# Unread 512-column products on TensorE around attention's first maxima and ahead of its first scores

## The chip, the cores and the metric

One core of a Trainium2 chip runs the whole kernel. The metric is the device time of one execution in microseconds (us). TensorE's clock is granted at one of two levels, 2.4 GHz (written 1.00 in the profile) or 1.2 GHz (written 0.50).

## The reference

A transformer block with adaptive layer norm, in float32, on `x` of 2 x 2048 tokens by 256. `mod` holds shifts, scales and gates computed from a condition vector. Cut to what matters:

```
h = layernorm(x) * (1 + ca) + sa
qkv = h @ qkv_w.T + qkv_b            # 16 heads of 16, rotary q and k
attn = softmax(q @ k.T * 16 ** -0.5)  # per batch and head, 2048 x 2048
x = x + ga * ((attn @ v) @ proj_w.T + proj_b)
h = layernorm(x) * (1 + cb) + sb
x = x + gb * (one of 8 relu experts, chosen by argmax of the gate logits)(h)
```

The softmax is exact: each query's maximum over its 2048 keys is found before the exponentials are taken.

## The kernel before, in words

Stages follow one another in one program: `front` (layer norm folded into weights, q, k, v, rotary), `attention`, `tail` (projection, second norm, routing), `experts`. Every engine has its own instruction stream, written out in full in Python, and the streams meet in semaphores. Within TensorE's stream the order is the order of the code; nothing is reordered by a planner.

Attention goes over 32 steps (`STEPS`). A step is four heads by 512 queries. For each step three kinds of products run on TensorE.

- **Maxima pairs** (`pair_product`, L1092 to L1104): two products at once, of 50 rows by 128 queries by 512 keys, in the two halves of the array (rows 0 to 49 and 64 to 113), into one of two PSUM buffers `PM`. VectorE reduces each pair to its maxima (`reduce_pair`, L1241 to L1245). 32 pairs make a step (`PAIR_TILES`). The operands are fp32r (the keys and queries split in a high and a low part, which is why they have 50 rows).
- **Scores** (`score_pair`, L1081 to L1090): `PS = K.T Q` for 128 keys by 512 queries, shifted by the maxima, into one of three PSUM banks (`SBANKS`). ScalarE takes the exponential of each (`exp_tile`, L1208 to L1213).
- **Values** (`value_products`, L1125 to L1139): eight instructions of 128 rows by 32 columns by 256, four of which share the array.

In the steady loop (`step`, L1174 to L1195) TensorE issues, for each of the 32 half groups of a step: one score pair two groups ahead (`OVER`), one maxima pair for the next step, and half of a group's value products. "Half group" below means this unit.

Before the loop there is a prologue (L1158 to L1172), and this is where the change lies. It has no scores to run beside, since the first step's maxima aren't known yet:

1. 32 pairs for step 0, each waiting until VectorE has freed its buffer (`maxima`, L1160).
2. `turn_shifts` (L1116 to L1123): four 128-column products that transpose the maxima, after VectorE's last reduction (L1252) and three small operations of GpSimd (L979 to L986). ScalarE copies the result (L1206), and SyncE moves it into `QE` (L860).
3. 14 early pairs of step 1 (`2 * EARLY`), the second of which waits for ScalarE's copy (`shifts_out`, L1166).
4. The first eight scores (`OVER` = 2 groups), and then step 0.

A wait stands in front of the instruction in TensorE's own stream, so whatever is written behind it waits too. The prologue starts once the last of `front` has finished.

Of the kernel before, what the change touches and what calls it, by code (L numbers as in the profile page):

```python
# [14 lines left out]
P = 128  # L15
# [13 lines left out]
CH = 512  # L29
# [673 lines left out]
def attention(nc, g):  # L703
# [8 lines left out]
    SBANKS = 3  # L712
# [6 lines left out]
    with ExitStack() as ctx:  # L719
        sem = open_sem(ctx, nc, "att")  # L720
        sb, ps = open_mem(ctx, nc, "att")
        K, QM = g.K, g.QM
# [17 lines left out]
        PS = [ps(f"PS{i}", [P, CH]) for i in range(SBANKS)]  # L740
# [36 lines left out]
        def shift_at(r, last):  # L777

            return SHIFT_AT - 2 * (SHIFT_GROUP + 1 - KT + EARLY) if last and r >= BODY - 2 else SHIFT_AT
# [5 lines left out]
        def pair_bank(r, at):  # L785
            return (FIRST + (PAIR_TILES + 1) * r + at) % 2

        def pair_number(s, at, shift):

            return PAIR_TILES + 2 * EARLY + PAIR_TILES * s + at - (1 if at > shift else 0) + 1  # L790
# [289 lines left out]
        def _(pe):  # L1080
            def score_pair(s, r, kt, ab):  # L1081

                if kt == 0 and ab == 0:
                    pe.wait_ge(shifts_placed, 16 * HEADS * (s + 1))
                for hh in range(2):
                    i = HEADS * kt + 2 * ab + hh
                    pe.wait_ge(exps, score_tile(s, i) - since_bank(i) + HELD)
                    rows = slice(64 * hh, 64 * hh + ROWS)
                    nc.tensor.matmul(PS[score_bank(i)][:], K[r % BODY // CHUNKS][rows, ab, kt * P:(kt + 1) * P],  # L1089
                                     QE[r % 2][rows, ab, :], start=True, stop=True).then_inc(scores, 1)  # L1090

            def pair_product(bank, r, it, n):  # L1092

                qt, ab, kc, u = n // 8, n // 4 % 2, n % 4, (r % BODY) // CHUNKS
                if n == 0:
                    if r > 0:
                        pe.wait_ge(queries_split, 2 * (BODY * it + r))
                    if r > 0 and r % CHUNKS == 0:
                        pe.wait_ge(keys_split, 2 * (2 * it + r // CHUNKS))
                for hh in range(2):  # L1100
                    rows = slice(64 * hh, 64 * hh + ROWS)
                    last = nc.tensor.matmul(PM[bank][:, hh, :], QM[r % 2][rows, ab, qt * P:(qt + 1) * P],  # L1102
                                            K[u][rows, ab, kc * CH:(kc + 1) * CH], start=True, stop=True)
                last.then_inc(max_products, 1)  # L1104

            def next_pair(s, r, it, last, at, ahead, n):

                shift = shift_at(r, last)
                number = pair_number(s, at, shift)
                if at == shift + 2:  # L1110
                    pe.wait_ge(shifts_out, s + 2)
                else:
                    pe.wait_ge(maxima, number - (1 if at == shift + 1 else 2) + AHEAD)
                pair_product(pair_bank(r, at), r + ahead, it, n)

            def turn_shifts(s, bank, pairs):  # L1116

                pe.wait_ge(shifts_ready, s + 1)
                pe.wait_ge(maxima, pairs - 1 + AHEAD)
                for qt in range(4):  # L1120
                    last = nc.tensor.matmul(PM[bank][:, 0, qt * P:(qt + 1) * P], mt[:, qt, :], identity[:],
                                            start=True, stop=True)
                last.then_inc(max_products, 1)  # L1123
# [33 lines left out]

            pe.sem_inc(pv_groups, SLOTS)  # L1158
            for n in range(PAIR_TILES):
                pe.wait_ge(maxima, n - 1 + AHEAD)  # L1160
                pair_product(n % 2, 0, 0, n)
            pe.wait_ge(ident_set, 3)
            turn_shifts(0, PAIR_TILES % 2, PAIR_TILES)
            for n in range(2 * EARLY):
                if n == 1:
                    pe.wait_ge(shifts_out, 1)  # L1166
                else:
                    pe.wait_ge(maxima, PAIR_TILES + n - (0 if n == 0 else 1) + AHEAD)
                pair_product((PAIR_TILES + 1 + n) % 2, 1, 0, n)
            for kt in range(OVER):  # L1170
                for ab in range(2):
                    score_pair(0, 0, kt, ab)  # L1172

            def step(it, r, last):  # L1174
                s = BODY * it + r
                final = last and r == BODY - 1
                issued = 0
                for j in range(KT):
                    for ab in range(2):
                        if j < KT - OVER:  # L1180
                            score_pair(s, r, j + OVER, ab)
                        elif not final:
                            score_pair(s + 1, r + 1, j - KT + OVER, ab)
                        ahead = 1 if j < KT - EARLY else 2
                        if ahead == 1 and not final or ahead == 2 and not (last and r >= BODY - 2):
                            n = 2 * (j + EARLY) + ab if ahead == 1 else 2 * (j - KT + EARLY) + ab
                            next_pair(s, r, it, last, issued, ahead, n)
                            issued += 1
                        if j == SHIFT_GROUP and ab == 1 and not final:
                            turn_shifts(s + 1, pair_bank(r, issued), PAIR_TILES * (s + 1) + 2 * EARLY + issued)  # L1190
                            issued += 1
                        value_products(s, r, it, j, ab)
                        at = 2 * (KT * (r - BODY + 2) + j) + ab - 2 * (SHIFT_GROUP + 2)
                        if last and 0 <= at < TB * KD:
                            first_projection(at)  # L1195
# [902 lines left out]
```

## Time and profile before

| | us |
|---|---|
| median of three runs | 1895.42 |
| the three runs | 1895.1 to 1900.64 |
| the profiled execution | 1896.42 |
| its span | 1894.7 |

| engine | busy share of the span |
|---|---|
| TensorE (PE) | 94% |
| VectorE (DVE) | 88% |
| ScalarE (ACT) | 75% |
| GpSimd (POOL) | 30% |

The span is the time from the first to the last instruction that the profiler saw; 1.72 us of the profiled execution lie around it. The line PEclk of the page gives the granted clock in 40 slices of 47.4 us. The page's list of groups shows attention's four large ones: 1024 reductions on VectorE (1245.5 us), 2048 exponentials on ScalarE (1112.3 us), 8192 value products (655.7 us) and 2048 score products (535.1 us) on TensorE. Times in the views are counted from the start of the span. A modelled matmul lasts from its issue until its result is there, so neighbouring ones overlap; the distance of two starts says what one really occupies.

### The profile page before, as it was taken

What the parts mean: (1) busy time and instruction counts of PE and PEld (TensorE: products, weight loads), DVE (VectorE), ACT (ScalarE), POOL (GpSimd) and SP (SyncE); (2) the same over time, 40 slices, a digit from 0 to 9 for tenths busy, and PEclk for the clock granted to TensorE, in tenths of its full rate; (3) what the DMA queues carried; (4) which work ended last, traced back from release to release, by engine and by line L of the source; (5) the groups of instructions that cost most, each with busy time, mean ns of one, the idle gap of its engine ahead of it and who ended that gap; (6) DMA issues with size and microseconds to landing.
All of it is one profiled execution on the core that took longest, in us unless ns stands there. A gap on an engine that the chain in (4) does not pass through costs nothing. (4 is left out here: it accounts for less than half of the span.)

```text
span 1894.7 us, 38505 instructions
## 1 busy us (share of the span) xinstructions
PE 1789.8 (94%) x15332; PEld 894.8 (47%) x15332; DVE 1658.5 (88%) x1803; ACT 1414.9 (75%) x2642; POOL 566.1 (30%) x406
## 2 busy tenths in 40 slices
PE   7976999999999999999999999999999994899997
PEld 4542333333333333333333333333333364899997
DVE  6779799999999999999999999999997475688886
ACT  1330788888888888888888888888888641688885
POOL 1115411151224115213411521331182015344442
PEclk8985899999999999999999999999999985899999
DMA  6766012331151133115113212521113733788873
GB/s 195 230 166 128 25 47 68 65 77 48 48 117 59 59 68 73 47 62 102 62 56 72 68 48 71 93 67 50 48 50 128 215 125 131 259 279 275 273 241 108
DMA packets 142660, 208.57 MB, mean 110 GB/s; under 512 B 42442, under 2 KB 87789, under 8 KB 140688
## 3 DMA queue, kind: packets, MB, share of 16 engines
q1 hardware_dynamic: 130608, 178.92, 33.1%
q0 software_dynamic: 7520, 18.80, 3.5%
q10 hardware_dynamic: 4352, 8.39, 1.3%
q8 instruction: 121, 1.98, 0.4%
q14 instruction: 59, 0.48, 0.1%
HBM read 122.10 MB, written 73.06 MB: 103 GB/s over the span
## 5 line engine op out<-in xcount | busy, mean ns | idle before, releaser
L1245 DVE TENSOR_REDUCE att_mx<-att_PM 128x2 f32<-128x1024 f32 x1024 | 1245.5, 1225 | 70.5 <-PE att_PM L1102 63.6
L1213 ACT ACTIVATE att_probs<-att_PS 128x512 f32<-128x512 f32 x2048 | 1112.3, 596 | 191.2 <-PE att_PS L1089 152.9
L1135 PE MATMUL att_PV<-att_probs,att_VU 128*32 128x256 f32 x8192 | 655.7, 392 | 7.8 <-ACT keep_sums L1234 6.2
L1089 PE MATMUL att_PS<-att_QE,K 50*128 50x512 f32 x2048 | 535.1, 498 | 1.9 <-ACT att_probs L1213 1.8
L1102 PE MATMUL att_PM<-K,QM 50*128 50x512 f32 x2048 | 439.4, 413 | 22.4 <-DVE att_mx L1245 15.0
L1089 PEld LDWEIGHTS att_PS<-att_QE,K 50*128 50x128 f32 x2048 | 203.4, 184 | 433.6 <-ACT att_probs L1213 410.5
L1135 PEld LDWEIGHTS att_PV<-att_probs,att_VU 128*32 128x32 f32 x8192 | 162.7, 108 | 368.9 <-issue 201.8
L979 POOL CAST att_mh<-att_m 128x16 fp32r<-128x16 f32 x32 | 6.3, 198 | 807.2 <-DVE att_m L1252 807.2
L1102 PEld LDWEIGHTS att_PM<-K,QM 50*128 50x128 f32 x2048 | 206.4, 191 | 44.8 <-DVE att_mx L1245 36.5
L576 POOL TENSOR_TENSOR QM<-QS,QM 16x1024 fp32r<-16x1024 f32 x62 | 146.5, 2363 | 8.5 <-POOL QM L995 6.1
L567 POOL TENSOR_TENSOR K<-KS,K 16x4096 fp32r<-16x4096 f32 x14 | 125.2, 8944 | 1.8 <-POOL K L1006 1.3
L1859 ACT ACTIVATE KS<-ffn_psh,ffn_b 128x256 f32<-128x256 f32 (+1 forms) x184 | 77.8, 496 | 44.2 <-PE ffn_psh L1955 43.6
L1811 POOL DMA_INDIRECT out<-QS,all_X x43 | 56.3, 1308 | 151.6 <-DVE QS L1896 139.3
L1919 DVE TENSOR_TENSOR ffn_hid_lo<-KS,ffn_hid_hi 128x512 fp32r<-128x512 f32 (+1 forms) x92 | 60.1, 654 | 15.7 <-ACT ffn_hid_hi L1859 14.8
L1955 PE MATMUL ffn_psh<-QM,keep_w_hi 128*128 128x256 f32 (+1 forms) x384 | 67.9, 281 | 1.4 <-ACT QM L1845 1.4
L1955 PE MATMUL ffn_psh<-QM,K 128*128 128x256 f32 (+1 forms) x528 | 64.6, 282 | 1.6 <-DVE K L1901 1.6
L1955 PEld LDWEIGHTS ffn_psh<-QM,K 128*128 128x128 f32 x528 | 63.6, 191 | 1.8 <-issue 1.8
L1969 PE MATMUL ffn_psy<-K,ffn_hid_hi 128*128 128x256 f32 x336 | 61.9, 286 | 0.0
L492 PE MATMUL front_psq<-front_xT,front_wf 128*128 128x512 f32 x128 | 58.6, 612 | 2.6 <-issue 2.6
L245 ACT ACTIVATE front_qk<-front_psq,front_bias_qk 128x512 f32<-128x512 f32 x32 | 22.0, 687 | 52.0 <-PE front_psq L492 52.0
L1955 PEld LDWEIGHTS ffn_psh<-QM,keep_w_hi 128*128 128x128 f32 x384 | 59.8, 194 | 1.8 <-ACT QM L1845 1.8
L1859 ACT ACTIVATE ffn_hid_hi<-ffn_psh,ffn_b 128x256 fp32r<-128x256 f32 (+1 forms) x138 | 58.2, 496 | 0.0
(217 smaller groups left out, 1598.9 us busy)
## 6 DMA issues: line engine op xcount, KB each, us to landing
H<-in_w SPq DMA_DIRECT2D x44, 1024.0 KB
routed_rows<-att_filling SPq DMA_DIRECT2D x32, 1088.0 KB, 4.3
att_QE<-QM SPq DMA_DIRECT2D x32, 512.0 KB, 3.1
QS<-qkT SPq DMA_DIRECT2D x186, 64.0 KB, 2.4
KS<-qkT SPq DMA_DIRECT2D x42, 256.0 KB, 9.0
qkT<-KS ACTq DMA_DIRECT2D x16, 512.0 KB, 4.9
all_X<-routed_rows SPq DMA_DIRECT2D x20, 258.0 KB
all_X<-in_x SPq DMA_DIRECT2D x4, 1024.0 KB, 9.8
```

What stands on the lines that cost most here:

```text
L492: last = nc.tensor.matmul(psq[:, odds, which, :], wf[b][:, k, n * P:(n + 1) * P], xT[q % 2][:, k, :], start=k == 0, stop=k == KD - 1)
L567: nc.gpsimd.tensor_tensor(keys[rows, :, :], stage[rows, :, :], keys[rows, :, :].bitcast(F32), ALU.subtract).then_inc(done, 1)
L576: nc.gpsimd.tensor_tensor(queries[rows, :, :], stage[rows, :, :], queries[rows, :, :].bitcast(F32), ALU.subtract).then_inc(done, 1)
L1089: nc.tensor.matmul(PS[score_bank(i)][:], K[r % BODY // CHUNKS][rows, ab, kt * P:(kt + 1) * P], QE[r % 2][rows, ab, :], start=True, stop=Tr ...
L1102: last = nc.tensor.matmul(PM[bank][:, hh, :], QM[r % 2][rows, ab, qt * P:(qt + 1) * P], K[u][rows, ab, kc * CH:(kc + 1) * CH], start=True, ...
L1135: last = nc.tensor.matmul(PV[32 * h:32 * h + VW, cols], VU[r // CHUNKS % 2][:, j, h, :], probs[:, j % SLOTS, h, cols], start=j == 0 and ha ...
L1213: nc.scalar.activation(probs[:, kt % SLOTS, h, :], PS[score_bank(i)][:], ACT.Exp).then_inc(exps, 1)
L1245: nc.vector.reduce_max(mx[:, r % 2, at:at + 2, kc], PM[bank][:], AX).then_inc(maxima, 1)
L1859: last = nc.scalar.activation(out[:, f, wide(k)], psh[p][:, f % 2, wide(k)], ACT.Relu, bias=b1[par][:, f:f + 1])
L1919: nc.vector.tensor_tensor(hid_part[1][:, two, wide(k)], hid[:, two, wide(k)], hid_part[0][:, two, wide(k)].bitcast(F32), ALU.subtract).the ...
L1955: last = nc.tensor.matmul(psh[f // 2][:, f % 2, wide(k)], w1_part[par][a][:, c, f * P:(f + 1) * P], hT[par][b][:, c, wide(k)], start=n == ...
L1969: last = nc.tensor.matmul(psy[par][:, s, :], hid_part[a][:, f, s * P:(s + 1) * P], w2_part[par][b][:, f, :], start=f == 0 and (a, b) == PA ...
```

## The change

A helper `fill(times)` is added to attention's TensorE stream. It issues products of `K[0][:, 0, 0:128]` (128 rows by 128 columns, the stationary side) with `K[0][:, 0, 0:512]` (512 columns, moving), fp32r, into the score banks `PS[0]` to `PS[2]` in turn. No instruction reads these results; the first scores overwrite them. It has no wait and raises no semaphore. It is called 31 times with 1 in the first maxima (ahead of every pair but the first, in front of its wait), 14 times with 1 in the early pairs (ahead of each), and once with 6 ahead of the first scores: 51 products in all.

```diff
@@ -1103,6 +1103,12 @@
                 last.then_inc(max_products, 1)
 
+            def fill(times):
+
+
+                for i in range(times):
+                    nc.tensor.matmul(PS[i % SBANKS][:], K[0][:, 0, 0:P], K[0][:, 0, 0:CH], start=True, stop=True)
+
             def next_pair(s, r, it, last, at, ahead, n):
@@ -1157,16 +1163,20 @@
             pe.sem_inc(pv_groups, SLOTS)
             for n in range(PAIR_TILES):
+                if n:
+                    fill(1)
                 pe.wait_ge(maxima, n - 1 + AHEAD)
                 pair_product(n % 2, 0, 0, n)
             pe.wait_ge(ident_set, 3)
             turn_shifts(0, PAIR_TILES % 2, PAIR_TILES)
             for n in range(2 * EARLY):
+                fill(1)
                 if n == 1:
                     pe.wait_ge(shifts_out, 1)
                 else:
                     pe.wait_ge(maxima, PAIR_TILES + n - (0 if n == 0 else 1) + AHEAD)
                 pair_product((PAIR_TILES + 1 + n) % 2, 1, 0, n)
+            fill(6)
             for kt in range(OVER):
                 for ab in range(2):
                     score_pair(0, 0, kt, ab)
```

## Rows read from the trace of the kernel before

**Rows 1.** The page: span, TensorE's busy time, its granted clock in 40 slices.

```profile
span 1894.7 us, 38505 instructions
...
PE 1789.8 (94%) x15332; PEld 894.8 (47%) x15332; DVE 1658.5 (88%) x1803; ACT 1414.9 (75%) x2642; POOL 566.1 (30%) x406
...
PEclk8985899999999999999999999999999985899999
```

**Rows 2.** Stretches of attention's start: length, busy times and counts, PEclk, DMA share, GB/s.

```profile
136.64:172.35 35.71, 25.04 (x64) 9.13 (x64) 34.88 (x31) 0.00 (x0) 16.30 (x16) 0.50 0.82 175
...
191.40:196.96 5.56, 3.96 (x12) 1.94 (x9) 1.41 (x2) 5.04 (x9) 5.48 (x2) 0.50 0.00 0
196.96:207.55 10.59, 10.59 (x60) 3.40 (x59) 5.69 (x5) 5.73 (x11) 6.05 (x1) 0.50 0.01 2
...
230.00:1240.00 1010.00, 999.41 (x9514) 378.36 (x9512) 963.12 (x815) 874.82 (x1619) 286.32 (x175) 1.00 0.27 68
```

**Rows 3.** Tile att_PM, 137 to 173 us: ns least/median/greatest, first and last start.

```profile
L1245 DVE TENSOR_REDUCE att_mx<-att_PM x32: 1216/1217/1227, 137.5 to 172.5; 128x2 f32<-128x1024 f32 x32
```

**Rows 4.** Timeline, one pair in the first maxima: start, length, idle and releaser.

```profile
139.88 0.80 PE L1102 MATMUL att_PM<-K,QM 50*128 50x512 f32 x2 [0.34 <-DVE att_mx L1245]
```

**Rows 5.** The tile att_PM, 177 to 192 us: the fourteen early reductions.

```profile
L1245 DVE TENSOR_REDUCE att_mx<-att_PM x14: 1216/1217/1226, 176.9 to 191.6; 128x2 f32<-128x1024 f32 x14
```

**Rows 6.** Timeline, 175 to 177 us: the turned shifts and the next pair.

```profile
175.03 1.09 PE L1121 MATMUL att_PM<-att_identity,att_mt 128*128 128x128 f32 x4 [2.68 <-POOL att_mt L986]
...
176.04 1.53 PE L1102 MATMUL att_PM<-K,QM 50*128 50x512 f32 x4
176.15 0.57 ACT L1206 CAST att_shift_rows<-att_PM 8x512 fp32r<-8x512 f32 x1 [45.80 <-PE att_PM L1121]
...
176.88 4.62 DVE L1245 TENSOR_REDUCE att_mx<-att_PM 128x2 f32<-128x1024 f32 x4 [2.87 <-PE att_PM L1102]
```

**Rows 7.** Timeline, 191 to 198 us: the first scores and exponentials.

```profile
191.20 1.05 PE L1089 MATMUL att_PS<-att_QE,K 50*128 50x512 f32 x3
191.91 1.28 ACT L1213 ACT_TABLE_LOAD   x1 [15.18 <-PE att_PS L1089]
193.20 5.14 ACT L1213 ACTIVATE att_probs<-att_PS 128x512 f32<-128x512 f32 x10
...
193.85 3.80 PE L1089 MATMUL att_PS<-att_QE,K 50*128 50x512 f32 x7 [1.60 <-ACT att_probs L1213]
...
196.96 1.12 PE L1102 MATMUL att_PM<-K,QM 50*128 50x512 f32 x2
```

**Rows 8.** Timeline, TensorE alone, 199 to 209 us: half groups at both clocks.

```profile
199.02 0.79 PE L1089 MATMUL att_PS<-att_QE,K 50*128 50x512 f32 x2
...
205.50 0.79 PE L1089 MATMUL att_PS<-att_QE,K 50*128 50x512 f32 x2
206.09 0.63 PE L1102 MATMUL att_PM<-K,QM 50*128 50x512 f32 x2
206.65 1.06 PE L1135 MATMUL att_PV<-att_probs,att_VU 128*32 128x256 f32 x8
207.64 0.50 PE L1089 MATMUL att_PS<-att_QE,K 50*128 50x512 f32 x2
...
208.87 0.50 PE L1089 MATMUL att_PS<-att_QE,K 50*128 50x512 f32 x2
```

**Rows 9.** Timeline, expert layers at the low clock: full-array fp32r products in a row.

```profile
1616.79 0.63 PE L1955 MATMUL ffn_psh<-QM,keep_w_hi 128*128 128x256 f32 x2
...
1617.43 0.63 PE L1955 MATMUL ffn_psh<-QM,keep_w_hi 128*128 128x256 f32 x2
```

**Rows 10.** Other stretches, columns as in Rows 2.

```profile
129.20:132.60 3.40, 0.04 (x1) 0.00 (x0) 3.40 (x4) 1.07 (x2) 0.00 (x0) 0.98 0.18 64
...
1569.40:1600.00 30.60, 19.21 (x84) 18.02 (x84) 12.63 (x55) 5.41 (x9) 17.47 (x19) 0.50 0.33 112
```

## The prediction, made before the changed kernel ran

> **What bounds the kernel now.** I began with the page: TensorE is busy 94% of the span, and its clock is granted at the high level in all but a few slices; one low place lies in the slices from 142 to 190 us, at the start of attention [rows 1]. Windows over that place tell what each stage does. From 136.64 us on the clock stands at 0.50 (1.2 GHz) through the first maxima, the early pairs, the first scores and the first 10.6 us of the steady loop; it rises at about 207.55 and stays up [rows 2]. From there on TensorE is the bound: 999.4 of 1010 us busy. So a microsecond that TensorE reaches the loop sooner or later is one microsecond of the end; I found no slack that would soak it up.
>
> Within the start the bound changes. In the first maxima VectorE is: 32 reductions, whose starts run from 137.5 to 172.5, one per 1.13 us, while TensorE has a pair ready in 0.80 and then sits 0.34 us waiting for VectorE [rows 3, 4]. The 14 early pairs are the same: (191.6 - 176.9) / 13 = 1.13 us each [rows 5]. Between the two lies a chain of single steps: turn, pair, reduction [rows 6]. In the first scores ScalarE is the bound, with a table load of 1.28 us and ten exponentials in 5.14 us without a gap [rows 7]. Only then does the low clock cost time: a half group takes (207.64 - 199.02) / 4 = 2.155 us, and 1.23 us at the high clock [rows 8]. From the first maxima pair of the loop at 196.96 to the score pair at 207.64 there are five half groups less one score pair.
>
> **What the change costs and may give, part by part.**
>
> Price of one unread product. The nearest full-array fp32r row has 256 columns: three instructions per 0.64 us (1616.79 to 1617.43) at the low clock, 0.213 each [rows 9]. With 512 columns that is 0.427 us at the low clock, half of it, 0.213, at the high one.
>
> The 31 in the first maxima and 13 of the 14 early ones. Does one fit between two pairs at the low clock? A pair holds the array, by the distance of starts, for 206.65 - 206.09 = 0.56 us until a full-height product can start [rows 8]. From a full-height product (two rounds of 0.427 for the values) to the next pair it is 207.64 - 206.65 = 0.99, so 0.14 beyond its columns [rows 8]. The unread product then takes 0.427 + 0.14 = 0.57, and the period on TensorE is 0.56 + 0.57 = 1.13 us, exactly VectorE's. The unread product stands in front of the wait, so it uses TensorE's idle time; what hides it is VectorE's reduction. I take nothing for it. If each of the 45 were 0.05 us too long (my reading error in each distance), that is +2.2 us, and I keep it for the range. If the clock is high all of it halves and fits easily. A gain isn't possible here, since VectorE is the bound.
>
> The one between the turn and the first early pair is open: GpSimd's result releases the turn, the pair starts at 176.04 and VectorE at 176.88 [rows 6]. The product goes in between: +0.5 us at the low clock (0.427 to 0.57). The next one, between this pair and the second, has the 1.13 us of the first reduction over it.
>
> The six ahead of the scores are open too. The last pair is issued when VectorE frees its buffer; behind it the first scores go at 191.20 at once, and their end releases ScalarE's table load at 191.91 [rows 7]. `place_shifts` has long been done, so nothing else holds them. Six products ahead: +6 x 0.427 = +2.56 us on the table load, on the exponentials, which have no gap, and so on the loop. At the high clock 1.28.
>
> What the clock could give. If TensorE stood at the high level from the first maxima to the loop, the turn and first pair would end 0.5 us sooner in spite of the product between them (1.85 us from 175.03 to 176.88 become about 1.3: turn 0.5, product 0.2, pair 0.5 [rows 6, 8]), the six cost 1.28, and the first score is ready in 0.50 rather than in about 0.7: ScalarE starts 0.35 us later. The loop then begins at 197.3; its first pair, values and the way to the next score pair take 1.03 rather than 2.06, the next four half groups 4.93 rather than 8.62. Sum: 0.35 - 1.03 - 3.69 = -4.4 us. This is the whole prize, 0.23% of the run.
>
> **Does the clock rise?** Rows against: 63% busy over 30 us in the routing did not raise it, and 70% did not in the first maxima [rows 2, 10]. The rise at 207.55 came after 10.59 us without a gap, about half of them full-height value products [rows 2, 8]. With the change the maxima too would have next to no gap, 1.13 of 1.13 us, but only 0.43 of that full-height; I lean to no rise there, and no more than lean. And between the six products and the loop lies ScalarE's stage: after the first scores 1.6 us with nothing, then one half-height product per half microsecond [rows 7]; a clock once raised has that to survive. It fell after the empty stretch from 129.20 [rows 10]. So I take it that it is low again, or still, at 197 us.
>
> The Trainium skill speaks the other way. TensorE: Matmul & The Clock Gate, Part 1 (What's actually happening), says that throttled is the default state and that activity releases it. Read simply, products in every gap are activity and the clock is high within the maxima; that is the second case below. The first maxima of before, 70% busy, do not bear such a simple reading out.
>
> **Cases, with times.** The sum stands against the profiled execution, 1896.42 us, 1.0 above the median of 1895.42; I give times by the median.
>
> 1. *Forecast: low clock throughout, as before.* +0.5 + 2.56 = +3.1 us: 1898.5. Its own range: down by half of the 4.7 us that the low clock costs in the loop if the six dense products bring the rise forward, up by 2.2 for pairs that just don't fit and by 1.5 for a rise that comes some 3 us later: 1896 to 1902.2. Chance 0.52.
> 2. *High clock from the maxima into the loop.* -4.4 us: 1891.0. For it: TensorE's gaps of 0.34 us in the maxima are gone. Against: the stage of ScalarE, which the products don't fill. Chance 0.20.
> 3. *High in the maxima, low again when the loop starts.* Only 0.35 us is lost and nothing won: 1895.8, give or take 1.5. Chance 0.17.
> 4. *Slower: the unread product shuts the array.* It takes all rows and columns. If it can't start before the pair is finished (0.80), and the pair's weights can't be loaded before it is finished (0.42 for 256 columns [rows 9], so 0.63), the period is 1.43 us rather than 1.13, 45 times: +13, and with the 3.1 of case 1 +16: 1911.5. It decides when the period passes 1.19 us, for (5.7 - 3.1) / 45 = 0.06. Against it stands the 0.56 us from pair to values. The same page, Part 3 (The mechanism), says that weight loads overlap running products only where their row groups differ, which speaks for it, since the unread product uses every row group. Chance 0.08.
> 5. *The products never reach the engine*, being read by nobody: 1895.4. Chance 0.03.
>
> **The numbers.** A measurement of this kernel can tell about 0.3%, 5.7 us, from no change. Slower than that: case 4 and the top of case 1, 0.13. Faster than that: no sum gets there, since the prize ends at 4.4; 0.04 for a prize that I read too small. Same: 0.83. The predicted time is case 1. The range runs from case 2 to the top of case 1, 1890.5 to 1902.5; it leaves out case 4 and some of each end.
>
> **What would show it.** In the changed kernel's windows PEclk should be 0.50 from 137 to 197 us; 1.00 anywhere before the early pairs makes case 2 or 3. Reductions of the first maxima one per 1.13 us; 1.2 or more makes case 4. ScalarE's table load at about 195.0 rather than 191.91, about 192.3 at the high clock. Half groups from about 200 us: 2.155 us each for some 8 to 10 us, or 1.23 from the first, which would make me wrong. The steady loop's half group should stay at 1.23; a change there has no place in this sum.

## The result, and the profile after

The changed kernel takes 1916.57 us (median of six runs, 1912.22 to 1918.35) against 1896.8 us for the kernel before (six runs, 1894.09 to 1900.64). The medians differ by 19.8 us; the ratio is 1.0095, 95% interval 1.0078 to 1.0112, so about 18 us slower, with 15 to 21 in the interval. The profiled execution has a span of 1915.2 us, 20.5 more than before.

The page first, to set beside [rows 1]:

```profile
span 1915.2 us, 38607 instructions
...
PE 1825.4 (95%) x15383; PEld 910.3 (48%) x15383; DVE 1662.6 (87%) x1803; ACT 1414.0 (74%) x2642; POOL 565.5 (30%) x406
...
PEclk8985599999999999999999999999999995899999
```

TensorE is 35.6 us busier, and the digits of the clock show one more low slice at attention's start. The stretches of attention's start, cut at the first pair, the end of the maxima, the first early pair, the six, the loop's first pair and the rise of the clock, with the columns of [rows 2]:

```profile
139.13:184.00 44.87, 44.87 (x95) 17.75 (x95) 37.41 (x31) 0.00 (x0) 16.31 (x16) 0.50 0.63 140
...
188.85:208.38 19.53, 19.53 (x43) 7.72 (x42) 15.94 (x13) 0.15 (x1) 19.00 (x5) 0.50 0.15 50
208.38:217.17 8.79, 7.19 (x18) 4.13 (x17) 1.23 (x1) 5.04 (x9) 6.93 (x1) 0.50 0.00 0
217.17:234.21 17.04, 17.04 (x96) 5.47 (x95) 9.35 (x8) 8.97 (x17) 0.00 (x0) 0.50 0.00 1
234.21:260.00 25.79, 25.59 (x246) 9.88 (x244) 23.83 (x22) 22.08 (x41) 6.29 (x6) 1.00 0.12 45
```

TensorE now has no idle time in the maxima: 44.87 us of 44.87, where it was busy 25.04 of 35.71 [rows 2]. Nor is there any in the early pairs. Yet the granted clock is 0.50 throughout, and rises only at 234.21. The timeline of one period shows why VectorE has to wait:

```profile
149.98 0.28 PEld L1110 LDWEIGHTS att_PS<-K 128*128 128x128 f32 x1 [0.44 <-issue]
149.98 0.79 PE L1110 MATMUL att_PS<-K 128*128 128x512 f32 x1
150.10 1.23 DVE L1255 TENSOR_REDUCE att_mx<-att_PM 128x2 f32<-128x1024 f32 x1 [0.22 <-PE att_PM L1102]
...
150.70 0.79 PE L1102 MATMUL att_PM<-K,QM 50*128 50x512 f32 x2
...
151.43 0.79 PE L1110 MATMUL att_PS<-K 128*128 128x512 f32 x1
151.54 1.23 DVE L1255 TENSOR_REDUCE att_mx<-att_PM 128x2 f32<-128x1024 f32 x1 [0.22 <-PE att_PM L1102]
```

Pair at 150.70, product at 151.43, next pair 0.72 us after that: from reduction to reduction (150.10 to 151.54) 1.447 us as the mean of the stretch, against 1.131. The bracket of VectorE, empty in the maxima of before, now says 0.22 us of waiting for TensorE; TensorE's own bracket, 0.34 us waiting for VectorE in [rows 4], is gone. The bound has changed sides. All 32 reductions agree (to compare with [rows 3]):

```profile
L1255 DVE TENSOR_REDUCE att_mx<-att_PM x32: 1225/1226/1227, 140.0 to 184.8; 128x2 f32<-128x1024 f32 x32
```

At the end of the early pairs stand the six:

```profile
208.38 2.93 PE L1110 MATMUL att_PS<-K 128*128 128x512 f32 x6
...
211.24 1.22 PE L1089 MATMUL att_PS<-att_QE,K 50*128 50x512 f32 x3
212.11 1.28 ACT L1223 ACT_TABLE_LOAD   x1 [23.12 <-PE att_PS L1089]
213.41 4.65 ACT L1223 ACTIVATE att_probs<-att_PS 128x512 f32<-128x512 f32 x9
```

The first score comes 2.86 us after the first of the six, and 3.6 us after the last pair at 207.66; it was 0.59 in [rows 7]. The table load keeps its length; the view cuts off the last of the ten exponentials, and the loop's first pair comes 5.06 us behind the table load's start, as it did before (5.05).

Where the time went, from the two traces, counted from the first maxima pair to the loop's first pair (60.32 us before, 78.04 after, so +17.72). The parts are counted between starts of VectorE's reductions:

| part | us |
|---|---|
| 31 periods of the first maxima, 35.08 to 44.85 | +9.77 |
| last reduction, turn and first early pair, 4.33 to 4.88 | +0.55 |
| 13 periods of the early pairs, 14.72 to 18.81 | +4.09 |
| the six, from the last reduction's start to the table load, 0.31 to 3.61 | +3.30 |

The profiled execution adds two things that I don't put down to the change, by the second traces below: its attention started 2.5 us later, and the loop stayed at the low clock for 17.0 us rather than 10.6, which comes to some 2.8 us by the half groups of [rows 8]. Together that is 23.0 us; at the end of attention the difference is 22.7, and 2.2 us came back in the tail.

### The profile page after: what moved, and what is told of

Read it like the earlier page. It is cut to its first block and busy times, and to the rows that moved or that the text cites. A ratio compares the mean times of both kernels' runs of the same rounds, so it can differ in the third digit from the quotient of the medians.

```text
span 1915.2 us, 38607 instructions
## 1 busy us (share of the span) xinstructions
PE 1825.4 (95%) x15383; PEld 910.3 (48%) x15383; DVE 1662.6 (87%) x1803; ACT 1414.0 (74%) x2642; POOL 565.5 (30%) x406
## 5 line engine op out<-in xcount | busy, mean ns | idle before, releaser
L1929 DVE TENSOR_TENSOR ffn_hid_lo<-KS,ffn_hid_hi 128x512 fp32r<-128x512 f32 (+1 forms) x92 | 60.2, 654 | 14.6 <-ACT ffn_hid_hi L1869 13.7
L1216 ACT CAST att_shift_rows<-att_PM 8x512 fp32r<-8x512 f32 x32 | 18.4, 573 | 55.8 <-PE att_PM L1127 55.8
```

The lines of the kernel that those rows point to most:

```text
L1929: nc.vector.tensor_tensor(hid_part[1][:, two, wide(k)], hid[:, two, wide(k)], hid_part[0][:, two, wide(k)].bitcast(F32), ALU.subtract).the ...
```

## The experiments

Each experiment's ratio is against the kernel before, run beside it on the same chip. The totals of one kernel spread by 10 to 16 us from lowest to highest where there are 19 or more runs of the kernel before, so the traces carry the argument where terms of a few us are at stake. "Period" is the mean distance of the reductions in the first maxima. The experiments have the short names e1 to e16. Edits are shown against the changed kernel in e1 to e5, e7, e8, e10 and e11, and against the kernel before, or an experiment that is named, in the others. Of all experiments only e2 keeps the six ahead of the scores; the line that takes them out is not shown each time. Dots mark other lines left out.

### The 45 among the pairs alone (e1)

```diff
-            fill(6)
```

> The 45 products among the pairs alone, without the six ahead of the scores. Theory F (form): a full-height product and a half-height pair can't overlap their weight loads, so each change of form costs 0.3 us beyond the 0.427 us of columns, and the period of a pair is 1.447 us at the low clock whatever stands later. Then first maxima +9.9 us, early pairs +4.2, turn +0.5: about +14.7, and 2.9 us less than the changed kernel: some 1912 us, ratio to before 1.008. Rival S (the six): if most of the loss comes from the six and a later rise of the clock behind them, this one is within 5 us of before.

1907.46 us against 1892.05, ratio 1.0085 (1.0059 to 1.011). Period 1.447, +9.78 us in the maxima, +14.56 from first pair to loop. So the 45 are the loss and the six a small part; rival S falls.

### The six alone (e2)

```diff
             for n in range(PAIR_TILES):
-                if n:
-                    fill(1)
...
             for n in range(2 * EARLY):
-                fill(1)
```

> The six products ahead of the scores alone. Theory F: they stand in a row, only the first changes form, so 6 x 0.427 + 0.3 = 2.9 us later for the first score, pairs at 1.13 us as before: about +2.9 us, ratio 1.0015, if the clock rises in the loop as late as before; up to 1.5 us more or less by the place of the rise. Rival S: over +10 us. A third reading (the six raise the clock early and it stays) would give -1 to -2 us and half groups of 1.23 us from the first.

1894.06 against 1892.05, ratio 1.0011 (0.9993 to 1.0029), which can't be told from one. The trace has periods of 1.131 and +3.15 us to the loop; then a low stretch of 6.2 us. The clock did not rise among the six.

### The same columns in the pairs' own form (e3)

```diff
-                    nc.tensor.matmul(PS[i % SBANKS][:], K[0][:, 0, 0:P], K[0][:, 0, 0:CH], start=True, stop=True)
+                    for hh in range(2):
+                        rows = slice(64 * hh, 64 * hh + ROWS)
+                        nc.tensor.matmul(PS[hh][:], K[0][rows, 0, 0:P], K[0][rows, 0, 0:CH], start=True, stop=True)
```

> 45 unread products as in the first of this call, but each replaced by two of 50 rows in the two halves of the array, as a pair has them: same columns per unit of time, twice the instructions, no change of form. Theory F: the distance of two such pairs is the 0.59 us seen between score pair and maxima pair, so a period of 1.19 us against VectorE's 1.13: +2.7 us for 45, about +3 in all, ratio 1.0015. Rival C (columns or instructions): any product of 512 columns between two pairs costs 0.72 us, period 1.45 or more, and the loss is that of the first kernel of this call or more.

1893.76 against 1892.05, ratio 1.0011 (0.9994 to 1.0028). This decides between form and columns. TensorE's timeline at the low clock:

```profile
149.85 0.79 PE L1102 MATMUL att_PM<-K,QM 50*128 50x512 f32 x2
150.45 0.63 PE L1112 MATMUL att_PS<-K 50*128 50x512 f32 x2
150.99 0.80 PE L1102 MATMUL att_PM<-K,QM 50*128 50x512 f32 x2
```

Twice the instructions, the same 512 columns, and 1.14 us for pair and product together, where full height takes 1.447. The period is VectorE's 1.131 again, so TensorE needs no more than that; theory F's 1.19 and +3 us were too high. From first pair to loop it is 60.75 us, +0.43. Look at the lengths: the product has 0.63, the pair 0.79. I read a length of 0.63 as weights that were already there when the product started, and 0.79 as weights that still had to be loaded: in the loop of before the weight loads (PEld) of a maxima pair start 0.43 us ahead of it, while those of a row of 0.79 start with it, as at 149.98 in the changed kernel.

```profile
199.18 0.34 PEld L1102 LDWEIGHTS att_PM<-K,QM 50*128 50x128 f32 x2
199.61 0.63 PE L1102 MATMUL att_PM<-K,QM 50*128 50x512 f32 x2
```

Rival C falls.

### 256 columns (e4)

```diff
-                    nc.tensor.matmul(PS[i % SBANKS][:], K[0][:, 0, 0:P], K[0][:, 0, 0:CH], start=True, stop=True)
+                    nc.tensor.matmul(PS[i % SBANKS][:, 0:256], K[0][:, 0, 0:P], K[0][:, 0, 0:256], start=True, stop=True)
```

> 45 full-height products of 256 instead of 512 columns, no six. Theory F (a fixed cost for each change of form, plus columns): period 1.447 - 0.213 = 1.234 us, so 45 x 0.10 = +4.6 us in maxima and early pairs. If instead the whole 0.72 us scaled with the columns, the period would be 0.72 + 0.36 = 1.08, below VectorE's 1.13, and nothing would be lost there. If the clock rose, both periods would be 1.13.

Period 1.233, as theory F said: 0.213 less for 256 columns less. So 1.447 is twice 0.427 of columns and 0.59 of something that doesn't depend on the product's columns. One run: 1895.98 us.

### Two per pair (e5)

```diff
-                    fill(1)
+                    fill(2)
```

> Two unread full-height products ahead of each pair instead of one, no six. Theory F (the cost hangs on each change between full and half height): two full-height products in a row differ by their 0.427 us of columns, so the period is 1.447 + 0.427 = 1.87 us at the low clock. Rival P (each full-height fp32r product pays for its own weight load and drain): 1.447 + 0.72 = 2.17 us. If the greater density makes the clock rise within the maxima, the period falls to VectorE's 1.13 us and the starts of the scores come near before's.

```profile
150.43 1.22 PE L1110 MATMUL att_PS<-K 128*128 128x512 f32 x2
151.58 0.79 PE L1102 MATMUL att_PM<-K,QM 50*128 50x512 f32 x2
152.30 1.22 PE L1110 MATMUL att_PS<-K 128*128 128x512 f32 x2
```

Period 1.873. From the two products at 150.43 to the pair it is 1.15 us, 0.43 more than with one, so two of the same form in a row cost columns only; rival P falls. TensorE was busy for all but 0.05 of 58.9 us in the maxima, and the clock stayed low. 1927.37 us in the one run.

### The form of the values (e11), and 32 weight columns (e10)

```diff
+                    for h in range(HEADS):
+                        nc.tensor.matmul(PS[i % SBANKS][32 * h:32 * h + 32, 0:P], K[0][:, 0, 32 * h:32 * h + 32].bitcast(F32),
+                                         K[0][:, 0, 0:P].bitcast(F32),
+                                         start=True, stop=True, tile_position=(0, 32 * h))
```

> 45 unread products in the form that the values have: four float32 products side by side, each 128 rows by 32 columns, here with 128 moving columns, which hold the array for the same 0.427 us; no six. My prediction took its 0.56 and 0.14 us from the neighbours of such products. Theory V (full height alone isn't the cost; the value form changes over in 0.27 us for both sides, the 128 by 128 form in 0.60): period 0.427 + 0.427 + 0.27 = 1.13 us and no loss in the maxima, so the step failed by the row it was read from. Theory H (any full-height product costs 0.60): period 1.447 again, +15 us.

```diff
+                    nc.tensor.matmul(PS[i % SBANKS][0:32, :], K[0][:, 0, 0:32], K[0][:, 0, 0:CH], start=True, stop=True,
+                                     tile_position=(0, 0))
```

> 45 unread fp32r products of 512 moving columns and full height, but with 32 instead of 128 weight columns (one column tile), no six. If the cost of the change of form is weight loading by columns, the product's own load shrinks by 96 columns, 0.08 us, and the period is 1.37 us; if the load of the next pair also no longer waits for the whole array, 1.13 to 1.29; if weight columns don't matter, 1.447.

```profile
149.28 0.79 PE L1102 MATMUL att_PM<-K,QM 50*128 50x512 f32 x2
150.01 0.65 PE L1111 MATMUL att_PS<-K 128*32 128x128 f32 x8
150.59 0.79 PE L1102 MATMUL att_PM<-K,QM 50*128 50x512 f32 x2
```

```profile
150.11 0.63 PE L1110 MATMUL att_PS<-K 128*32 128x512 f32 x1
150.68 0.79 PE L1102 MATMUL att_PM<-K,QM 50*128 50x512 f32 x2
151.40 0.63 PE L1110 MATMUL att_PS<-K 128*32 128x512 f32 x1
```

The first fence is of the value form, the second of 32 weight columns. Periods 1.307 and 1.287: between both theories of the first. The second lies in the range 1.13 to 1.29, but not for the reason given there, since the pair's own length is still 0.79. The value form took 1909.49 us against 1900.4, ratio 1.005 (1.0033 to 1.0066); the other one 1911.97 in one run. The two distances tell more than the sum. From pair to product it is 0.72 us in all full-height forms, as in the changed kernel. From product to pair it is 0.72 with 128 weight columns and 0.57 with 32. So the parts of a period are:

- 0.427 of columns for the pair and 0.427 for the product,
- 0.13 to 0.14 at each change of form (it can be seen in the loop of before, maxima pair to values and values to scores, 0.56 and 0.99 us in [rows 8]; the clock rose within that 0.99, and the row below gives 1.01 wholly at the low clock, from 204.49 to the scores at 205.50),
- some 0.16 for loading 128 weight columns, once for the pair and once for the product, since it was not done ahead at a change of form in any of these rows; 0.02 where the product has only 32.

```profile
204.49 1.08 PE L1135 MATMUL att_PV<-att_probs,att_VU 128*32 128x256 f32 x8
```

Sum for the changed kernel: 0.85 + 0.27 + 0.32 = 1.44, measured 1.447; for the value form 0.85 + 0.27 + 0.18 = 1.30, measured 1.307. The Trainium skill, TensorEngine Tiling (Array Packing), Key Properties, says that a switch of tiling mode drains the engine. In e3, e4, e5 and e10 the time is lost at the change of form, which agrees; whether the engine was drained in full these rows can't tell, since a matmul's end is modelled. That the weight loads come on top, 0.16 us each, is from the rows here.

### Can the products carry a high clock? (e6 to e9, e12)

Six float32 products at the end of the stage before, in TensorE's idle time, and no others:

```diff
+            pe.wait_ge(rotated, TURNS * (ROUND - 1) + 1)
+            for i in range(6):
+                nc.tensor.matmul(psx[:, i % 2, :], wf[1][:, 0, 0:P], xT[1][:, 0, :], start=True, stop=True)
```

> No product among the pairs; instead six unread float32 products of 512 columns at the end of the stage before attention, in TensorE's 7.4 us of idle time there (into a bank that nobody reads any more), so that the engine stands still only some 2 us before the first pair. Theory K (the clock fell because of that empty stretch and the pairs alone, 0.8 us in 1.13, can keep it): granted clock 1.00 in the maxima, pairs ready in 0.5 us, loop at the high clock or not according to the gap at 172 us and the scores. Theory L (the pairs alone can't keep it): 0.50 again within the maxima, all as before, time within 2 us of before.

```profile
137.74:140.40 2.66, 1.24 (x6) 0.48 (x6) 2.12 (x2) 0.00 (x0) 2.66 (x4) 1.00 0.85 303
140.60:197.70 57.10, 39.01 (x100) 15.57 (x101) 50.12 (x46) 5.55 (x10) 34.85 (x22) 0.50 0.52 112
197.77:219.00 21.23, 21.23 (x120) 6.87 (x119) 11.68 (x10) 11.13 (x21) 6.06 (x1) 0.50 0.00 1
```

The pairs began at the high clock and lost it 2.8 us later, with nothing but pairs and their gaps in between. 1893.25 against 1889.26, ratio 1.0004 (0.9985 to 1.0023). Theory L. The low stretch in the loop was 21.2 us here.

The same with the 45:

```diff
+            pe.wait_ge(rotated, TURNS * (ROUND - 1) + 1)
...
-            fill(6)
```

> The six float32 products at the end of the stage before, and the 45 full-height products among the pairs, none ahead of the scores. If the clock is high when the maxima begin and stays (theory K, helped by the 45), the change of form costs half as much: period on TensorE 0.72 us, under VectorE's 1.13, no loss in the maxima; before's time, or 3 to 5 us less if the clock also stands in the loop. If the clock falls in spite of them, the period is 1.447 and the loss is that of the 45 alone, +15 us.

It fell at 140.9, 1.6 us after the first pair; period 1.422; 1902.38 us, ratio 1.0063 (1.0043 to 1.0083). With more full-height products in the gap before the turn (8), under ScalarE's table load (6 into the value bank `PV`, which nobody reads before the loop, by the helper `fill_values`) and behind each later score (one of 256 columns):

```diff
             pe.wait_ge(ident_set, 3)
+            fill(8)
             turn_shifts(0, PAIR_TILES % 2, PAIR_TILES)
...
+                        if i == 2:
+                            fill_values(6, CH)
+                        if i > 2:
+                            fill_values(1, CH // 2)
```

> As the one with front products and 45, and in addition eight full-height products in TensorE's 2.7 us gap before the turn, six into the value bank behind the third score (under ScalarE's table load) and one of 256 columns behind each later score of the first eight. If the high clock can be carried from the stage before into the loop, this is the version that does it: 1.00 from 137 us on, half groups of 1.23 us from the first, 4 to 5 us less than before (more where before stays low longer in the loop). If the clock falls on the way, +15 to +20 us.

1903.44 us, ratio 1.0056 (1.0037 to 1.0075); some 11 us, and 11.8 in the trace at the loop's 33rd reduction, less than the +15 to +20 given to a falling clock.

```profile
184.00:189.20 5.20, 5.20 (x15) 3.78 (x13) 1.67 (x3) 0.31 (x1) 2.37 (x5) 0.50 0.02 5
189.40:196.00 6.60, 5.78 (x20) 2.34 (x20) 6.14 (x6) 0.07 (x1) 6.33 (x3) 1.00 0.33 111
196.20:206.00 9.80, 9.80 (x21) 4.10 (x23) 8.82 (x8) 0.00 (x0) 9.62 (x2) 0.50 0.07 18
```

Here the answer on "one per pair" stands in two rows. The clock rose at 189.3, behind the eight in a row, the turn and one more product. There VectorE was the bound again (period 1.13), and one product per pair was hidden; but TensorE was then busy only 5.78 of 6.60 us, and the clock fell at 196.1.

Two per pair, after six in the gap before the turn, nothing in the first maxima (e9; against the kernel before, and without the lines for the six under the table load, which are those of e8):

```diff
             pe.wait_ge(ident_set, 3)
+            fill(6)
             turn_shifts(0, PAIR_TILES % 2, PAIR_TILES)
             for n in range(2 * EARLY):
+                fill(1 if n == 0 else 2)
```

> Nothing in the first maxima; six full-height products in the 2.65 us gap before the turn (2.56 us, hidden), one after the turn and two ahead of every other early pair, six into the value bank under ScalarE's table load. One product per pair let a raised clock fall after 6.8 us in the earlier run. If two per pair hold it: raised by about 180 us, period 0.93 of 1.13, scores at the high clock, and a loop that is high from the start or soon after: up to 5 us less than before. If it doesn't rise behind the gap, two per pair cost 0.74 us each, 13 times, +9.7 us, and the two switches more.

```profile
171.94:175.10 3.16, 3.16 (x10) 2.28 (x9) 1.71 (x3) 0.00 (x0) 1.08 (x4) 0.50 0.00 0
175.20:190.90 15.70, 15.70 (x62) 7.07 (x61) 14.62 (x13) 0.67 (x2) 14.68 (x5) 1.00 0.18 61
190.90:195.60 4.70, 4.50 (x13) 2.13 (x12) 1.30 (x2) 4.69 (x9) 4.62 (x2) 1.00 0.01 3
195.69:212.60 16.91, 16.91 (x96) 5.60 (x95) 9.11 (x8) 8.90 (x17) 7.16 (x1) 0.50 0.00 0
```

High for 20 us, and low from the loop's first pair, for 17: just before it stand five scores of half height with nothing beside them. 1903.86 us, ratio 1.0024 (1.0005 to 1.0043). With all of it from the stage before on (e12: the products of e6, four ahead of the first pair, two ahead of each later one, eight in the gap, six under the table load):

```diff
             for n in range(PAIR_TILES):
+                fill(2 if n else 4)
...
             pe.wait_ge(ident_set, 3)
+            fill(8)
```

> The most that unread products can do here: six float32 products at the end of the stage before, four ahead of the first pair, two ahead of every later one, eight in the gap before the turn, six under the table load. If two per pair hold a high clock, 1.00 from the maxima to the scores, period 1.13, and a time 2 us above to 5 us below before's. If the clock falls within the maxima, the period becomes 1.87 and up to +33 us are lost, less where the dense stretches raise it again.

```profile
139.02:173.64 34.62, 34.62 (x125) 14.99 (x125) 34.08 (x31) 0.00 (x0) 15.26 (x14) 1.00 0.81 169
```

High from the first pair to 198.7, 0.8 us into the loop, then low for 13.7 us; 1900.18 us against 1900.4, ratio 1.0007 (0.9973 to 1.0041). So with two per pair the high clock stood, with one it fell, and in both kernels with two it fell right behind the bare scores. Two of the ten runs took 1923 and 1926 us. The trace, a run of 1908.33 us, shows what can add to a total: its clock also fell for 20.5 us at 1427.5, deep in the loop, where the code is that of before.

### Second traces, and products behind the scores (e13 to e16)

Both kernels again, with no edit:

> The kernel before, unchanged, for a second trace. If the length of the low stretch in the loop and the start of attention are matters of the single execution, both differ here from the first trace (10.6 us from the loop's first pair to the rise, first maxima pair at 136.6) by several us; if they belong to the kernel, they are within 0.5 us.

> The changed kernel, unchanged, for a second trace. The period must be 1.447 us again and the first score 17 to 18 us later after the first maxima pair than before's 54.6 us, since that is the change. The low stretch in the loop (17.0 us in the first trace) should differ if it is chance; if the change causes it, it is long again, 15 to 20 us.

```profile
197.89:208.42 10.53, 10.53 (x60) 3.39 (x59) 5.63 (x5) 5.73 (x11) 6.05 (x1) 0.50 0.01 2
```

```profile
139.19:217.23 78.04, 73.90 (x158) 31.00 (x158) 56.61 (x47) 5.62 (x10) 43.89 (x25) 0.50 0.41 93
217.23:223.46 6.23, 6.23 (x36) 1.99 (x35) 3.21 (x3) 3.55 (x7) 0.00 (x0) 0.50 0.00 0
```

Here are the low stretches of the loop: 10.5 us again for before, but 6.2 us for the changed kernel, which had 17.0. From first pair to loop both repeat to 0.01 us: 60.31 and 78.04. Over the 17 traces that have a low stretch in the loop it had between 5.6 and 23.5 us (23.5 with the half-height products of e3) without an order in the edits. The start of attention lay at 139.1 and 139.2 us for the changed kernel, at 136.6 and 137.6 for before; but two kernels whose stage before attention is the same code lie at 136.3 (e9) and 140.0 (the six alone). I take both for chance of the single execution; for the start, two traces a side are thin. Both traces of the changed kernel have two low stretches of 3.4 us in the stage before (from 77 and from 118 us in the first), and neither trace of before has them; but e16 has them too, with the code of before in that stage.

```diff
                         if i == 2:
                             fill_values(6, CH)
+                        if i > 2:
+                            fill_values(1, CH)
```

This is the one-per-score kernel (e13) against e9; the other (e14) has `fill_values(2, CH)`. Six such products stand behind score three in both.

> As the kernel with six in the gap, two per early pair and six under the table load, and one more full-height product of 512 columns behind each of the scores four to eight. At the high clock a score and such a product take about 0.85 us instead of ScalarE's 0.51, so five of them cost 1.7 us. If the clock then stands in the loop, half groups of 1.23 us from the first save 0.43 of the low stretch (10 to 17 us of it: 4 to 7 us), 2 to 5 us net. If it falls again before or in the loop, 2 us slower than before.

One per score: the clock fell at 197.5, just ahead of the fourth of them; 1902.72 us, ratio 1.0015 (0.9982 to 1.0047).

> The same with two per score: 1.07 us per score, five cost 2.8 us. Two per pair held the clock among the pairs, so by that it should hold here: high in the loop, 1 to 4 us net less than before. If the clock is low all the same in the loop's first microseconds, 3 us more than before, and the unread products have no form left in which they win.

Two per score: the six in the gap did not raise the clock this time, and the early pairs ran at 1.873 us (+9.6). But it rose at 207.75 under the table load and then never fell; 1906.86 us against 1901.1, ratio 1.0006 (0.998 to 1.0033). The six in the gap are too few to count on, and the runs say so too: they fall in two groups, four at 1895.3 to 1896.5 us with a mean granted clock of 0.965 or more and six at 1906.3 to 1911.3 with 0.957 to 0.959, where the trace belongs. That the four are those in which the six in the gap raised the clock is my reading; no trace of one was taken.

The last two: two per score put into the kernel with front products and two per pair (e15, here against e12), and the part at the scores alone, with no product among the pairs (e16, which is the kernel before with these lines and the six).

```diff
                         if i == 2:
                             fill_values(6, CH)
+                        if i > 2:
+                            fill_values(2, CH)
```

> The kernel with front products, two per pair and six under the table load, and two more behind each of the scores four to eight, which in the last call kept the clock high into the loop. If it is high all the way: first maxima pair to the 33rd reduction of the loop in 103 us against 106.4 us before, so 3 us less; ratio 0.998 to 0.999, hardly to be told in totals. If the clock falls anywhere among the pairs: +0.74 us for each pair behind that place.

> Before, with six full-height products under ScalarE's table load and two behind each of the scores four to eight; nothing among the pairs, no six ahead of the scores. If the six raise the clock under the table load (as in the two traces where they stood there at the low clock), the scores cost 2 to 4 us more and the loop is high from the first: -4.6 us against a low stretch of 10.6 us, more against a longer one. Net -2 to +1 us. If the clock rises late, each of five scores costs 0.6 to 1.1 us: +3 to +5 us.

```profile
139.00:173.00 34.00, 34.00 (x124) 15.18 (x123) 34.00 (x31) 0.00 (x0) 12.83 (x13) 1.00 0.77 157
173.00:193.00 20.00, 18.92 (x74) 8.96 (x72) 16.54 (x16) 3.00 (x5) 18.01 (x8) 1.00 0.14 48
193.00:201.00 8.00, 8.00 (x43) 3.37 (x42) 2.26 (x2) 5.49 (x10) 7.92 (x2) 1.00 0.01 2
201.00:240.00 39.00, 38.55 (x370) 14.64 (x372) 37.31 (x33) 33.95 (x63) 8.17 (x7) 1.00 0.08 30
```

Every row of the kernel with all of it says 1.00. From first maxima pair to the 33rd reduction of the loop: 103.05 us against 106.43, the 3.4 us that were expected. The totals don't show it: 1887.13 against 1891.14, ratio 1.0 (0.9975 to 1.0025). Nine of the twelve runs lie at 1884.7 to 1887.9 us with a mean granted clock of 0.978 to 0.981, the other three at 1897.3, 1897.6 and 1911.2 with 0.971, 0.970 and 0.964; picking the nine afterwards would not be a measurement. With the part at the scores alone the distance is 105.48, in the range that was given: six under the table load raised the clock at 195.7, and the loop ran high from its first pair. 1890.08 us, ratio 1.0003 (0.9984 to 1.0023).

## Why the prediction was wrong

**The bounds of the kernel before, and what a lost microsecond costs: right.** VectorE in the maxima, the chain over the turn, ScalarE in the scores, TensorE in the loop; a microsecond lost before the loop was one at the end, to within what the clock does behind it. That VectorE would stay the bound of the maxima was wrong.

**The step that failed: "0.56 + 0.57 = 1.13 us, exactly VectorE's".** I took the pair's 0.56 us in [rows 8] from a maxima pair that follows a score pair of the same form, whose weights are loaded ahead. The mark stood in the rows I quoted: that pair has a length of 0.63, the lone pair of [rows 4] 0.80. In the maxima a full-height product stands before each pair, so the pair's own load of 0.16 us is exposed. The product's is, too: the values in [rows 8] have 32 weight columns, the unread product has 128. Two missed terms of 0.16 make 0.32, and 1.13 + 0.32 = 1.45; over 44 periods that is the +13.9 us of the table, for which I took nothing. Everything else of that sum held: columns 0.427 (the six differ by that), change of form 0.13 to 0.14. And I gave "0.05 us" as my reading error for a distance that was short by 0.32.

**The cover was exactly used up.** My sum had no slack at all, 1.13 under 1.13. I said what hides the products, and put only 2.2 us in the range for its loss. A cover that fits to the last 0.01 us should have had a far larger chance of failing than 0.08.

**Case 4, at 0.08, is what happened.** It named the mechanism and the place, priced it by full completion of each (1.43 us, measured 1.447) and multiplied: +13. Measured: +9.77, +4.09 and the switches of turn and six, 17.7 in all, against its sum of 16; its 1911.5 us were 5 short of the median of 1916.57. Its point of decision, 1.19 us, was passed. Its reason is another one, and that its period came so near is in part luck: it added 0.80 and 0.63 for two completions, the rows have 0.72 and 0.72. As far as the modelled ends tell, the pair's weights don't wait for the product's completion: in e10 their load starts 0.57 us behind a product that lasts 0.63. The rule on weight loads that case 4 leaned on is borne out only in part. The loads were exposed at each change of form, but full-height products in a row, which use the same rows of the array, stand 0.43 us apart in e5 and hide theirs; there the measurement decides.

**The turn and the six:** +0.5 forecast, +0.55 measured; +2.56 forecast, +3.30 measured. In e2, where the pairs keep their period, it is +3.15, and two changes of form and two exposed loads make 0.27 + 0.32 = 0.59 of it.

**The clock: right in the outcome, the reason only in part shown.** It stayed at 0.50 in the maxima, though gapless, and in e5 even two products per pair didn't raise it. Case 2 didn't come about with one per pair where the clock had been raised first: it fell after 1.6 us in e7 and after 6.8 in e8. The stage of ScalarE, which I named as what a raised clock has to survive, was not put to the test in the changed kernel, whose clock was never high there; in e9 and e12 the clock fell right behind it, and in e15, with two products beside each score, it didn't. Why the mixtures of e5 and of the changed kernel left it low is not shown.

**The prize:** -4.4 us forecast, -4.7 of it for a loop at the high clock. e14, e15 and e16 had that: from the loop's first pair to its 33rd reduction 41.3 us against 46.1, so -4.8. e15's attention gained 3.4 us, net of 2.7 us for the products behind the scores.

What is open: why the low stretch in the loop is sometimes 6 and sometimes 23 us long, which I didn't try to steer, and what the clock answers to.

## What to carry to other kernels

Before work is put into an idle gap of TensorE, look at what stands on both sides: a change between half-height and full-height products cost 0.13 us at the low clock here and exposed the weight load behind it, 0.16 us for 128 weight columns, so a filler between two products should have their form. Take distances only from rows whose neighbours have the same form as in the new order; the length of the instruction (0.63 or 0.79 us here, for 512 columns at the low clock) tells whether its weights were there. And a sum that finds the cover used up to the last hundredth isn't a zero: its failure belongs among the likely cases.

## What was not expected of the hardware

- Gapless TensorE work didn't suffice for the high clock: 44.9 us in the changed kernel and 58.9 us with two products per pair, at 0.50 throughout. In some places it rose just behind products in a row: behind eight in the gap before the turn in e8, behind six there in e9 and e13 but not in e14, behind six under ScalarE's table load in e8, e14 and e16. Behind six ahead of the scores it didn't, in three traces (e2 and both of the changed kernel). The Trainium skill, TensorE: Matmul & The Clock Gate, Part 1 (What's actually happening), has activity releasing the throttle; these rows do not bear that out for these two mixtures of half and full height. The loop mixes both as well and did raise the clock, 5.6 to 23.5 us behind its first pair.
- Where the clock stood mattered: two products per pair left a low clock low (e5) and a high one high for 54 us (e12). One per pair lost a high clock after 6.8 us (e8) or 1.6 us (e7), the pairs alone after 2.8 us (e6).
- The reductions of the first maxima took 1226 ns (median) rather than 1217 with full-height products beside them, and 1212 with the half-height ones of e3.
